# The middle blocks of a feed-forward stage as a hardware loop instead of written out

## The chip, the cores and the metric

The kernel runs on one core of a Trainium2 chip. The metric is the device time of one execution in microseconds (us). Each of the five engines (PE for matmuls, DVE, ACT, POOL, and SP, which only issues transfers here) has its own instruction stream, read by its own sequencer; semaphores order the streams among each other.
## The reference

An input x of shape (2, 2048, 256) in float32 goes through four residual stages, each on a layer-normalised x. Here they are called A, B, C and D:

```
x = x + A(layernorm(x))    # rmsnorm, product with w_qkva, sigmoid gate, scan over time, times q
x = x + F(layernorm(x))    # B: feed-forward
x = x + C(layernorm(x))    # second-order linear attention, 16 heads, then @ W_o
x = x + F(layernorm(x))    # D: the same feed-forward

def F(x, W1, b1, W2, b2):                       # W1 (1024, 256), W2 (256, 1024)
    h = einsum('bsd,fd->bsf', x, ternary(W1)) + b1
    h = gelu(h)                                 # exact, not the tanh form
    return einsum('bsf,df->bsd', h, ternary(W2)) + b2
```

The change touches the code of stage B alone.

## The kernel before

x stays in on-chip memory (`xres`) for the whole run. Rows are taken in blocks of 512, so each of the two batches b has `NBLK` = 4 blocks, and stage B works through eight half-iterations: block i of batch 0, block i of batch 1, then the next i. One *iteration* below is one i, with both batches.

In a half-iteration PE makes eight groups of 128 hidden columns, f = 0 to 7. `up` (L695, L696) is four matmuls of 512 columns for one group, into one of two PSUM banks (`HB`). ACT applies GELU (L758) and then copies the high part (`hid_hi`, L747); DVE subtracts to get the low part (`hid_lo`, L802). `down` (L708, L710), the second product, runs one half-iteration later: eight parts of eight matmuls of 256 columns, woven between the ups from f = 2 on, the last two parts after f = 7. After f = 3 come the eight transposes (L169) of the next half-iteration's normalised rows.

Waits that matter around the change. `up` of group n waits until the GELU of group n-2 has freed its bank (`gelu_done`). GELU waits for its group's matmuls (`h_ready`), for the low part made four groups earlier (`hlow_done`), and, at f = 0, for `out_ready`. The first `down` part waits for all eight low parts of the half-iteration before it. Every count is the sum of a start value and i times a constant, so with i known when the program is built it is a constant.

Each engine's order in stage B comes from one helper, `steps` (L623 to L629), which calls the engine's `iteration` for i = 0, 1, 2, 3 and writes all four out, so that every count and every address of `xres` is a constant. Stage A is built by another helper, `stage_loop` (L270 to L279): it writes i = 0 and i = 3 out and puts i = 1 and i = 2 in a hardware loop `Fori`, in which i is a register of each engine. The rows of stage A therefore show a two-pass loop on the same engines. Stages C and D are written out.

Of the kernel before, what the change touches and what calls it, by code (L numbers as in the profile page):

```python
# [18 lines left out]
NBLK = T // BLK  # L19
# [13 lines left out]
def hybrid_kernel(nc, x_d, gamma_d, wqkva_d, wq_d, wk_d, wv_d, wo_d, w1_d, b1_d, w2_d, b2_d, out_d):  # L33
# [13 lines left out]
    with outer:  # L47
# [558 lines left out]
        def feed_forward(tag, stage, w1t, w2t):  # L606
            with ExitStack() as st:
# [15 lines left out]
                def steps(iteration, tail):  # L623

                    def run(eng):
                        for i in range(NBLK):
                            iteration(i, i == 0, i == NBLK - 1)
                        tail()
                    return run  # L629

# [1071 lines left out]
```

How the kernel before makes its waits and increments, by code:

```python
            def dve_statistics(self, dve, b, i, n):  # L138
                for c in range(CH):
                    nc.vector.bn_stats(ln_stats[:, b, c, :], rows(b, i, c)).then_inc(self.stats_done[b], 1)
                dve.wait_ge(self.stats_done[b], START + (n + 1) * CH)
                nc.vector.memset(ln_filler[:, :], 0.0)
                for c in range(CH):
                    nc.vector.bn_aggr(ln_moments[:, b, c, :], ln_stats[:, b, c, :]).then_inc(self.moments_done[b], 1)
# [1 line left out]
            def pool_rstd(self, pool, b, n):  # L147
                pool.wait_ge(self.moments_done[b], START + (n + 1) * CH)
                nc.gpsimd.tensor_tensor(ln_vare[:, b, :], ln_moments[:, b, :, 1], ln_eps[:, :],
                                        ALU.add).then_inc(self.vare_done[b], 1)
                pool.wait_ge(self.vare_done[b], START + n + 1)
                nc.gpsimd.tensor_tensor(ln_rstd[:, b, :], ln_vare[:, b, :], minus_half[:, :],
                                        ALU.pow).then_inc(self.rstd_done[b], 1)
# [1 line left out]
            def dve_normalise(self, dve, b, i, n, factor):  # L156
                dve.wait_ge(self.transposed[b], START + n * DC)
                for c in range(CH):
                    nc.vector.tensor_scalar(self.xn[:, b, c, :], rows(b, i, c), ln_moments[:, b, c, 0:1],
                                            factor[:, b, c:c + 1], ALU.subtract, ALU.mult)\
                        .then_inc(self.normalised[b], 1)
```

## Time and profile before

| what | value |
|---|---|
| median of 3 runs | 1068.14 us (1068.07 to 1070.59) |
| the profiled execution | 1068.14 us |
| its span, first to last instruction | 1066.4 us |
| stage A, about 0 to 126 us of the span | 126 us |
| stage B, about 126 to 266 us | 140 us |
| stages C and D | 800 us |
| mean granted clock of PE | 0.988 of full speed |

Between the span and the execution's own time lie 1.7 us, which no row shows. Busy time of PE counts matmuls, which overlap one another (a matmul of 512 columns is shown with 0.39 us, and the next starts 0.23 us after it), so the view to read is where each matmul starts, and what sits before the few late ones.

### The profile page before, as it was taken

Reading aid. Unit: us, or ns where it says so; the run is one execution under the profiler, and the core shown is the slowest. Engines: PE = TensorE matmul, PEld = TensorE weight load, DVE = VectorE, ACT = ScalarE, POOL = GpSimd, SP = SyncE. Lnnn points to the kernel's source line nnn. Section 1 sums busy time; section 2 is a strip of 40 time slices with the busy share of each in tenths; the row PEclk is TensorE's granted clock in tenths of the full one; section 3 lists DMA queues with packets and bytes.
Section 4 is the critical chain, followed back from the end, with each engine's and each line's share of the span. In section 5 each row is a group of like instructions: output and inputs, shape, how many; then the busy total and the mean of one; then the engine's idle time right before and its main releaser. Section 6 shows DMA issues by size and latency. Waiting matters only on the chain.

```text
span 1066.4 us, 42059 instructions
## 1 busy us (share of the span) xinstructions
PE 1014.1 (95%) x19150; PEld 917.4 (86%) x19150; DVE 652.2 (61%) x1315; ACT 470.0 (44%) x875; POOL 128.8 (12%) x114
## 2 busy tenths in 40 slices
PE   6799689998999999999999999999999999999998
PEld 5677579898999899899999998999999888888897
DVE  6999698776253564554555465555546446857773
ACT  4222376664334343343343343344344334546663
POOL 2315264122000000000000000000000000112130
PEclk9999899999899999999999999999999999999999
DMA  9100240002142332342343334234233332300101
GB/s 296 54 1 0 56 182 1 1 1 80 68 134 85 123 117 82 103 139 84 101 122 102 102 103 117 91 96 132 91 96 126 104 121 92 105 18 30 41 30 50
DMA packets 60687, 92.74 MB, mean 87 GB/s; under 512 B 7008, under 2 KB 50400, under 8 KB 59488
## 3 DMA queue, kind: packets, MB, share of 16 engines
q1 hardware_dynamic: 60512, 90.07, 26.7%
q8 instruction: 150, 2.46, 1.0%
q14 instruction: 25, 0.20, 0.1%
HBM read 48.63 MB, written 41.42 MB: 84 GB/s over the span
## 4 chain that ended last, share of the span: by engine, by line
PE 72%; DVE 1%; issue 1%; ACT 1%; POOL 0%; POOLq 0%
PE bank L213 7%; PE bank L214 6%; PE bank L215 6%; PE bank L1085 6%; PE bank L1111 5%; PE bank L1096 5%; PE bank L1145 3%; PE bank L1133 3%; PE bank L1122 3%; PE bank L1075 3%; PE bank L1146 3%; PE bank L1147 3%; PE bank L1161 3%; PE bank L1179 3%; PE bank L1180 3%; PE bank L1076 3%
## 5 line engine op out<-in xcount | busy, mean ns | idle before, releaser
L1503 DVE STREAM_TRANSPOSE k<-kt 128x512 f32<-128x512 f32 x64 | 43.4, 697 | 111.0 <-ACT kt L1362 60.7
L1367 ACT COPY qt<-bank 128x512 f32<-128x512 f32 x64 | 37.6, 587 | 151.6 <-PE bank L215 151.6
L1524 DVE TENSOR_TENSOR state_s<-bank,state_s 128x256 f32<-128x256 f32 x124 | 46.6, 419 | 73.0 <-ACT ut L1380 71.0
L1362 ACT COPY kt<-bank 128x512 f32<-128x512 f32 x64 | 37.6, 587 | 119.7 <-PE bank L215 119.7
L213 PE MATMUL bank<-ln_xhi,wk_hi 128*128 128x256 f32 x256 | 76.9, 301 | 4.1 <-POOL state_z L1019 3.4
L1145 PE MATMUL bank<-wo_hi,ot_hi 128*128 128x256 f32 x256 | 75.5, 295 | 0.0
L213 PE MATMUL bank<-ln_xhi,wq_hi 128*128 128x256 f32 x256 | 75.4, 294 | 0.0
L214 PE MATMUL bank<-ln_xlo,wk_hi 128*128 128x256 f32 x256 | 73.5, 287 | 1.0 <-issue 1.0
L215 PE MATMUL bank<-ln_xhi,wk_lo 128*128 128x256 f32 x256 | 73.3, 287 | 0.2 <-issue 0.2
L1517 DVE TENSOR_TENSOR state_z<-bank,state_z 128x512 f32<-128x512 f32 x62 | 39.9, 686 | 53.1 <-PE bank L1133 53.0
L1146 PE MATMUL bank<-wo_lo,ot_hi 128*128 128x256 f32 x256 | 72.2, 282 | 0.0
L214 PE MATMUL bank<-ln_xlo,wq_hi 128*128 128x256 f32 x256 | 72.2, 282 | 0.0
L1147 PE MATMUL bank<-wo_hi,ot_lo 128*128 128x256 f32 x256 | 72.1, 282 | 0.0
L215 PE MATMUL bank<-ln_xhi,wq_lo 128*128 128x256 f32 x256 | 72.1, 281 | 0.0
L802 DVE TENSOR_TENSOR B_hid_lo<-B_hidden,B_hid_hi 128x512 fp32r<-128x512 f32 x64 | 56.3, 902 | 25.5 <-ACT B_hid_hi L747 25.4
L1096 PE MATMUL bank<-qt,state_s 64*64 64x64 f32 x2048 | 69.3, 221 | 1.9 <-issue 1.8
L1414 ACT ACTIVATE D_hidden<-bank,b_sb 128x512 f32<-128x512 f32 x64 | 44.2, 691 | 60.3 <-PE bank L1162 60.3
L1096 PEld LDWEIGHTS bank<-qt,state_s 64*64 64x64 f32 x2048 | 64.4, 135 | 6.4 <-issue 2.5
L1100 PE MATMUL bank<-qt,state_z 64*64 64x64 f32 x2048 | 69.7, 221 | 0.0
L1100 PEld LDWEIGHTS bank<-qt,state_z 64*64 64x64 f32 x2048 | 64.6, 135 | 0.6 <-issue 0.3
L708 PE MATMUL bank<-w2t,B_hid_hi 128*128 128x256 f32 x256 | 63.8, 285 | 0.5 <-DVE B_hid_lo L802 0.5
L710 PE MATMUL bank<-w2t,B_hid_lo 128*128 128x256 f32 x256 | 63.5, 283 | 0.0
(155 smaller groups left out, 2956.5 us busy)
## 6 DMA issues: line engine op xcount, KB each, us to landing
k_rows_scratch<-k SPq DMA_DIRECT2D x32, 512.0 KB, 2.9
k<-k_rows_scratch SPq DMA_DIRECT2D x128, 128.0 KB, 3.5
u_rows_scratch<-sc_and_k SPq DMA_DIRECT2D x31, 512.0 KB, 3.1
landed<-u_rows_scratch SPq DMA_DIRECT2D x124, 128.0 KB, 3.1
out_dram<-xres SPq DMA_DIRECT2D x16, 256.0 KB, 2.1
xres<-in_L_attn_a_x_dram SPq DMA_DIRECT2D x4, 512.0 KB, 7.3
w_nat<-in_L_ffn_W_dram SPq DMA_DIRECT2D x2, 1024.0 KB, 8.9
xres<-in_L_attn_a_x_dram SPq DMA_DIRECT2D x2, 1024.0 KB, 15.2
```

The source lines that it names most:

```text
L213: nc.tensor.matmul(out, w_hi, x_hi, start=(k == 0), stop=False)
L214: nc.tensor.matmul(out, w_hi, x_lo, start=False, stop=False)
L215: return nc.tensor.matmul(out, w_lo, x_hi, start=False, stop=(k == last_k))
L708: nc.tensor.matmul(dst, hid_hi[:, b, f, c * P:(c + 1) * P], w2t[:, f, :], start=(f == 0), stop=False)
L710: last = nc.tensor.matmul(dst, hid_lo[:, b, f, c * P:(c + 1) * P], w2t[:, f, :], start=False, stop=(f == FC - 1))
L802: nc.vector.tensor_tensor(hid_lo[:, b, f, :], hidden[:, f % 4, :], hid_hi[:, b, f, :].bitcast(FP32), ALU.subtract).then_inc(hlow_done, 1)
L1085: last = nc.tensor.matmul(bank[bank_of[h]][half(b), p * CHUNK:(p + 1) * CHUNK], keys(p, h, b), qt[half(h), j // 2 % 2, p, j % 2, b, :], st ...
L1096: last = nc.tensor.matmul(bank[UB[b][p // 4]][half(h), u_cols(p, 0)], state_s[half(h), b, p, :], qt[half(h), j // 2 % 2, p, j % 2, b, :], ...
L1100: last = nc.tensor.matmul(bank[OB[b]][half(1 - h), cols], state_z[half(h), b, p, :], qt[half(h), (j - 1) // 2 % 2, p, (j - 1) % 2, b, :], ...
L1145: nc.tensor.matmul(dst, ot_hi[:, p, :], w[0], start=(p == 0), stop=False)
L1146: nc.tensor.matmul(dst, ot_hi[:, p, :], w[1], start=False, stop=False)
L1147: last = nc.tensor.matmul(dst, ot_lo[:, p, :], w[0], start=False, stop=(p == PAIRS - 1))
```

## The change

`steps` now writes i = 0 out, puts i = 1 and i = 2 in a hardware loop, and writes i = 3 out, for every engine that uses it (PE, ACT, DVE, POOL). SP's program has no such loop.

```
                     def run(eng):
-                        for i in range(NBLK):
-                            iteration(i, i == 0, i == NBLK - 1)
+                        iteration(0, True, False)
+                        with eng.Fori(1, NBLK - 1) as i:
+                            iteration(i, False, False)
+                        iteration(NBLK - 1, False, True)
                         tail()
                     return run
```

The matmuls and other operations, their order and their buffers are the same, and the arithmetic too. What differs is the form in which i reaches them. On ACT, this is the start of iteration i = 1 before (the casts end i = 0; `B_hlow`, `B_h`, `B_out0` are the semaphores `hlow_done`, `h_ready`, `out_ready[0]`):

```order
L770 CAST wk_hi<-B_wqk_raw 128x512 x3
L758 ACTIVATE B_hidden<-bank,b_sb 128x512 [waits B_hlow,B_h,B_out0]
L758 ACTIVATE B_hidden<-bank,b_sb 128x512 [waits B_hlow,B_h]
L747 CAST B_hid_hi<-B_hidden 128x512 [waits B_gelu]
L758 ACTIVATE B_hidden<-bank,b_sb 128x512 [waits B_hlow,B_h]
```

and this is the same place now, two lines lower in the file:

```order
L772 CAST wk_hi<-B_wqk_raw 128x512 x3
L627 UNCONDITIONAL_BRANCH
L627 ISA
L757 ISA [waits B_out0]
L759 REGISTER_ALU [waits B_h]
L760 ACTIVATE B_hidden<-bank,b_sb 128x512 [waits B_hlow]
L757 REGISTER_ALU
L759 REGISTER_ALU [waits B_h]
L760 ACTIVATE B_hidden<-bank,b_sb 128x512 [waits B_hlow]
L749 CAST B_hid_hi<-B_hidden 128x512 [waits B_gelu]
```

Register instructions stand between the operations, and for batch 0, f = 0, the wait for the matmuls sits on one of them, ahead of the GELU. On PE the end of the loop body is this (the last of the down matmuls, then the test of i, then the first up of i = 3, which is written out):

```order
L712 MATMUL bank<-w2t,B_hid_lo 128x256
L627 REGISTER_ALU
L627 COMPARE_AND_BRANCH
L697 MATMUL bank<-ln_xhi,w1t 128x512 [waits B_gelu,ln_low_done0]
```

and the branch leads back once to this, the start of the body:

```order
L627 UNCONDITIONAL_BRANCH
L627 ISA
L694 REGISTER_ALU [waits ln_low_done0]
L697 MATMUL bank<-ln_xhi,w1t 128x512 [waits B_gelu]
L698 MATMUL bank<-ln_xlo,w1t 128x512
L697 MATMUL bank<-ln_xhi,w1t 128x512
L698 MATMUL bank<-ln_xlo,w1t 128x512
L694 REGISTER_ALU
L697 MATMUL bank<-ln_xhi,w1t 128x512 [waits B_gelu]
```

One copy of an iteration fewer stands in each engine's program, and every instruction behind stage B stands that much earlier in it. PE's copy has 208 matmuls, each with its weight load.

## Rows read from the trace of the kernel before

**Rows 1.** The page: busy us, share of the span and instructions of each engine.
```profile
PE 1014.1 (95%) x19150; PEld 917.4 (86%) x19150; DVE 652.2 (61%) x1315; ACT 470.0 (44%) x875; POOL 128.8 (12%) x114
```

**Rows 2.** Busy time by stretch (columns in the first line): a half-iteration of stage B.
```profile
core 0: us, PE busy (x) PEld busy (x) DVE busy (x) ACT busy (x) POOL busy (x), PEclk, DMA share, GB/s
174.05:190.12 16.07, 16.07 (x107) 14.42 (x105) 13.35 (x27) 10.37 (x18) 3.95 (x3) 1.00 0.00 1
```

**Rows 3.** Waits, 175 to 239 us: us in total, times, longest.
```profile
ACT B_hidden L758 <- PE bank L696: 14.3, 20, 1.6
ACT B_hidden L758 <- issue: 8.5, 4, 2.1
PEld bank L695 <- ACT B_hidden L758: 1.4, 4, 0.3
```

**Rows 4.** Timeline at a half-iteration's start: start, us, engine, line, operation.
```profile
174.75 0.40 PE L696 MATMUL bank<-ln_xlo,w1t 128*128 128x512 f32 x1
...
175.23 0.69 ACT L758 ACTIVATE B_hidden<-bank,b_sb 128x512 f32<-128x512 f32 x1 [2.12 <-issue]
...
175.67 0.39 PE L696 MATMUL bank<-ln_xlo,w1t 128*128 128x512 f32 x1
175.97 0.19 PEld L695 LDWEIGHTS bank<-ln_xhi,w1t 128*128 128x128 f32 x1 [0.34 <-ACT B_hidden L758]
```

**Rows 5.** Timeline, stage A: the gate behind its matmuls, written out, then in loop.
```profile
24.85 0.39 PE L215 MATMUL bank<-ln_xhi,wa_lo 128*128 128x512 f32 x1
...
25.28 0.60 ACT L460 ACTIVATE gate<-bank 128x512 f32<-128x512 f32 x1 [1.90 <-PE bank L215]
...
70.14 0.39 PE L215 MATMUL bank<-ln_xhi,wa_lo 128*128 128x512 f32 x1
...
70.64 0.60 ACT L460 ACTIVATE gate<-bank 128x512 f32<-128x512 f32 x1 [5.20 <-PE bank L215]
```

**Rows 6.** Line 275, stage A's loop: duration ns min/median/max, first and last start us.
```profile
L275 PEldq FUSED_REGOPS  x2: 59/59/59, 39.7 to 64.2; - x2
L275 PEldq COMPARE_BRANCH  x2: 83/164/246, 63.9 to 85.2; - x2
L275 DVEq COMPARE_BRANCH  x2: 50/56/63, 67.6 to 88.8; - x2
```

**Rows 7.** Line 692 on PE's sequencer, 186 to 190 us (columns as rows 6).
```profile
L692 PEldq EVENT_SEMAPHORE  x1: 51/51/51, 188.0 to 188.0; - x1
```

**Rows 8.** Transfers in four stretches (46:67, 67:88, 158:190, 354:358): packets, MB.
```profile
q8 instruction: 1, 0.02, 0.4%
...
DMA packets 0, 0.00 MB, mean 0 GB/s; under 512 B 0, under 2 KB 0, under 8 KB 0
...
q8 instruction: 2, 0.03, 0.4%
...
q8 instruction: 1, 0.02, 2.0%
```

**Rows 9.** The page, transfers by queue over the run: packets, MB, share.
```profile
q8 instruction: 150, 2.46, 1.0%
```

**Rows 10.** PE's waits behind no other engine, 268 to 1066 us; then one of them.
```profile
PE bank L1085 <- issue: 2.3, 2, 1.5
PE bank L1096 <- issue: 1.8, 3, 1.3
...
357.50 0.28 PE L1085 MATMUL bank<-qt,kt 64*64 64x64 f32 x4 [1.48 <-issue]
```

**Rows 11.** A long wait of PE in stage B, and the stretch behind it (columns: rows 2).
```profile
141.83 0.50 PE L695 MATMUL bank<-ln_xhi,w1t 128*128 128x512 f32 x1 [2.50 <-ACT B_hidden L758]
...
142.50:145.90 3.40, 2.92 (x12) 2.20 (x11) 3.40 (x3) 1.56 (x3) 3.40 (x3) 0.50 0.57 234
```

**Rows 12.** Timeline, 162 to 164 us: the last normalise, and the transposes that read it.
```profile
162.07 1.38 DVE L160 TENSOR_SCALAR ln_xn<-xres,ln_moments,ln_rstd 128x256 f32<-128x256 f32 x1
...
163.77 0.38 PE L169 MATMUL bank<-ident,ln_xn 128*128 128x128 f32 x2
```

## The prediction

> **What bounds the kernel now.** I read the busy shares first, then the stretches of stage B, its waits, and one half-iteration's start. PE is busy 95% of the span [rows 1]. In the middle of stage B it is busy all the time: a half-iteration takes 16.07 us, of which PE is busy 16.07, at the full clock (2.4 GHz), with ACT at 10.4 and DVE at 13.4 us [rows 2]. So only what makes a matmul start later costs time there. The waits show one such place: in 64 us PE's weight load waits four times for a GELU, 1.4 us in all, once per half-iteration [rows 3]. The timeline shows it: the last matmul of up 0 starts at 174.75 and lasts 0.40, so it ends at 175.15; the GELU follows at 175.23, ends at 175.92, and up 2, which needs that bank back, starts at 175.97. The matmul before it started at 175.67, and the steady step between such matmuls is 0.23 us, so up 2 is 0.07 us late [rows 4]. This chain has no slack: each nanosecond added between up 0 and the end of the first GELU makes PE late by as much, once per half-iteration. The other GELUs have down parts between the ups, and ACT waits for PE there (20 times, 14.3 us [rows 3]), so they have room.
>
> **What the change adds.** No operation is removed, added or moved. Four things change.
>
> *Waits and addresses through registers.* The loop covers i = 1 and i = 2, four half-iterations. On ACT, in the two halves of batch 0, the wait for up 0 stands on a register instruction, and the GELU is sent off behind it. Stage A's loop has just that, and its written-out part has not. Written out, the last matmul ends at 24.85 + 0.39 = 25.24 and the gate starts at 25.28, 0.04 us later; in the loop it ends at 70.53 and the gate starts at 70.64, 0.11 us later [rows 5]. Difference 0.07 us. For f = 0 in stage B before, the distance is 175.23 - 175.15 = 0.08 us [rows 4], since three waits are already divided there, so the difference may be as small as 0.03. I take 0.05 us for two halves = 0.1 us. In the two halves of batch 1 the register instruction waits for the down products, done before up 0; I take nothing. Bounds: 0 (the register instruction hides in the 0.04 to 0.08 that a wait costs anyway) and 0.12 in all four halves, 0.5 us.
>
> On DVE register instructions stand before the normalises, the statistics and the adds. In steady iterations ACT and PE do not wait for DVE at all [rows 3], and its idle time per half is 16.07 - 13.35 = 2.7 us [rows 2]. One place is tight, at the loop's entry: the last normalise ends at 162.07 + 1.38 = 163.45 and the transposes that read it start at 163.77 [rows 12], 0.32 us of room. Entering the loop costs DVE's sequencer one or two register steps (PE's took 59 ns [rows 6]), and it reads ahead while the add before still runs. I take 0; bounds 0 and 0.2 us, once. POOL is busy 3.9 us of 16 and has room.
>
> *The jump back.* It is taken once per engine. In stage A PE's branch took 246 ns when taken and 83 when not, with a register step of 59 ns behind it; DVE's took 63 and 50 ns [rows 6]. A sequencer step costs time only if the sequencer is not ahead of its engine. PE's carried out its wait for the up that runs at 190.12 [rows 2] already at 188.0 [rows 7], 2.1 us ahead. The jump takes from 63.9 to 64.2 + 0.06, about 0.4 us [rows 6], and the first register wait in the body perhaps 0.1: hidden, with 1.6 us to spare. ACT at this place waits 2.1 us for up 0 anyway [rows 3] and jumps inside that wait. On DVE the branch, and as much again for register steps, lies in its 2.7 us. Cost 0; the upper bound, no cover at all, is PE's 0.4 us.
>
> *Instruction loads.* PE's instructions arrive in packets on queue q8, 150 for 2.46 MB [rows 9], 16 KB each; with 2 x 19150 matmuls and weight loads [rows 1] that is about 255 instructions a packet. The loop of stage A (two steps of 52 matmuls, some 220 instructions) loaded one packet during its first pass and none in its second: the stretch 67:88 has no packets at all, of any engine [rows 8]. So a jump back across one packet's boundary loaded nothing. The body in stage B is 208 matmuls with their weight loads and some twenty register instructions, about 440 instructions; in the same stretch before, 158:190, two packets came [rows 8], so the body spans two boundaries and the jump goes back over both. No row shows that. I take it as free as well, from the nearest row; its price if it is not is the second rival's.
>
> *Code behind stage B moves.* One copy of about 420 instructions less, so all of the packets' boundaries fall elsewhere in stages C and D. There PE waits at times behind no engine at all, for instance 1.48 us at 357.50, with one load in that stretch [rows 8, 10]; the two longest rows of this kind make 2.3 + 1.8 = 4.1 us over the 800 [rows 10]. Where the boundaries fall decides which loads come late. The sum has no direction; all of it could go (-4) or as much be added (+4). I take 0, and a spread of 1.5 to 2 us. The three runs themselves differ by 2.5.
>
> Sum: 0.1 + 0 + 0 + 0 = +0.1 us. The profiled execution took 1068.14, which is also the median of the runs, so 1068.2; the small terms' bounds are 0 and 0.5 + 0.2 + 0.4 = 1.1 us, mostly above, so I say 1068.3.
>
> The Trainium skill has a rule against the change: the page "Runtime: NRT & Kernel Launch", section "Instruction fetch mechanics", says that a taken branch whose target is not in the current window of two pages forces a fetch of that page before the engine goes on. By that rule the jump of stage A could stay inside the window, as the trace shows, and that of stage B, two pages back, could not; it would make the second or the third rival below of my forecast.
>
> **The rivals.**
>
> 1. *Forecast*: all of it hidden, 1068.3. For it: the second pass of stage A's loop loads nothing [rows 8], and PE's sequencer is 2.1 us ahead [rows 2, 7]. Against: the longer body.
>
> 2. *The jump back reloads, and is partly covered.* PE's sequencer must fetch a packet before it goes on. The nearest price is a load that came late in stage C, 1.48 us of idle PE where little cover was [rows 10]. So 0 to 1.5 us, 1069.8 at most. The next two boundaries in the body lie some 150 or more instructions on, at 0.12 us and more for a pair of them, and are loaded in time. For it: the body spans two boundaries. Against: nothing in stage A's second pass had to be loaded again.
>
> 3. *The other side: the reload is long enough for the clock to fall.* Place: PE, the start of i = 2. After its idle 2.50 us before 141.83 PE ran at half clock (1.2 GHz) for the 3.40 us from 142.50, its 2.92 us of busy time worth half of that at full clock [rows 11]: a loss of about 1.7 us of the 3.4. If the reload leaves PE idle as long as that wait did, the cost is 2.5 + 1.7 = 4.2 us: 1072.5. It decides when the fetch takes more than the 2.1 us of lead and 2.5 us on top, 4.6 us in all. Against: a late load in stage C showed at most 1.5 us.
>
> 4. *The boundaries in stages C and D.* They fall better, fewer late loads: about -4 us, 1064.3. Or worse: +4, 1072.3. In between, it only shifts the forecast inside its spread.
>
> **How the numbers follow.** About 0.3%, 3.2 us, is what a measurement of this kernel tells from no change. The forecast with small shifts from rival 4: 0.68. Rival 2: 0.15, also inside. Rival 3: 0.08, slower. Rival 4 with a gain over 3.2 us: 0.05; with a loss over 3.2 us: 0.04. So faster 0.05, slower 0.12, within 0.3% 0.83. The range: below, the forecast less 2 us of shift, 1066.3; above, rival 2 at its full price and one more late load of 1.2, 1071.0. That leaves out about 2 in 10.
>
> **What would show it.** The profile after should have half-iterations of 16.1 us through i = 1 and i = 2; the first GELU of batch 0's halves 0.03 to 0.1 us later behind its matmuls; one taken branch on PE of about 250 ns with no gap on PE behind it; and one pass of the loop without any packet on q8, so 148 packets or fewer instead of 150 (with rival 2 they are loaded again and the count stays). PE's waits behind no engine in stages C and D will sit at other places. I am wrong if PE shows a gap over 1 us at the start of i = 2, if a half-iteration inside the loop is over 16.4 us, which would mean that the register waits take PE's lead away, or if the late loads in stages C and D change by more than 3 us.

## The result, and the profile after

The looped kernel took 1078.07 us (median of 9 runs, 1074.74 to 1083.16), the kernel before beside it 1068.65 us (9 runs). The ratio is 1.0087, 95% interval 1.0066 to 1.0106: slower by about 9 us, where 1068.3 and no change had been predicted. The profiled execution took 1076.05 us. Its page has the same work as rows 1 and 9, a span 7.9 us longer, and one packet of instructions less:

```profile
span 1074.3 us, 42245 instructions
PE 1014.4 (94%) x19150; PEld 917.1 (85%) x19150; DVE 652.4 (61%) x1315; ACT 469.4 (44%) x875; POOL 129.4 (12%) x114
...
q8 instruction: 149, 2.44, 1.0%
```

The changed place itself behaves as foreseen. Two half-iterations in the loop, by stretch, as in [rows 2] (16.07 us there):

```profile
core 0: us, PE busy (x) PEld busy (x) DVE busy (x) ACT busy (x) POOL busy (x), PEclk, DMA share, GB/s
173.50:189.50 16.00, 16.00 (x106) 14.40 (x105) 13.16 (x27) 10.35 (x18) 3.94 (x3) 1.00 0.01 2
189.50:205.50 16.00, 16.00 (x105) 14.37 (x104) 12.50 (x25) 10.35 (x18) 3.93 (x3) 1.00 0.00 0
```

The instructions of the loop's line, as in [rows 6], show the branch on TensorE taken at 187.2 in 242 ns, and passed at 219.3 in 83:

```profile
L627 PEldq FUSED_REGOPS  x2: 59/59/59, 154.3 to 187.5; - x2
...
L627 PEldq ALU_OP  x2: 32/32/32, 187.1 to 219.2; - x2
L627 PEldq COMPARE_BRANCH  x2: 83/162/242, 187.2 to 219.3; - x2
```

Transfers of 158:190 and of 190:222, as in [rows 8]: two packets on q8 in the first pass, none of any queue in the second, so the jump over two boundaries loaded nothing again.

```profile
q8 instruction: 2, 0.03, 0.4%
...
DMA packets 0, 0.00 MB, mean 0 GB/s; under 512 B 0, under 2 KB 0, under 8 KB 0
```

The time is lost some 90 us and more behind the loop's end. From TensorE's first matmul of stage B to its first of stage C it took 139.1 us before and 138.0 after; from there to the end of the span 799.9 before and 808.7 after, +8.8. These are the first matmuls of stage C, before and after:

```profile
266.53 0.58 PE L213 MATMUL bank<-ln_xhi,wk_hi 128*128 128x256 f32 x1 [3.45 <-POOL state_z L1019]
```
```profile
265.67 0.39 PE L213 MATMUL bank<-ln_xhi,wk_hi 128*128 128x256 f32 x1 [3.45 <-POOL state_z L1021]
```

The following are TensorE's waits in stages C and D that the profile puts behind no other engine ("issue"). [rows 10] showed 2.3 and 1.8 us as the two largest rows of the kernel before; the looped kernel has:

```profile
PE bank L1087 <- issue: 6.1, 4, 2.0
PE bank L1102 <- issue: 2.8, 4, 1.5
...
PE bank L1147 <- issue: 1.4, 1, 1.4
PE bank L214 <- issue: 1.3, 1, 1.3
PE bank L1098 <- issue: 0.9, 2, 0.5
```

They make 12.5 us; in the kernel before all such waits make 5.9. One of the two longest is a row of the timeline. Behind it, and behind one like it that ends at 607, the clock is at half (1.2 GHz) for 3.4 us (two stretches, columns as above):

```profile
315.49 0.50 PE L1087 MATMUL bank<-qt,kt 64*64 64x64 f32 x17 [1.96 <-issue]
```
```profile
317.20:320.60 3.40, 3.40 (x24) 3.18 (x26) 0.25 (x2) 0.00 (x0) 0.00 (x0) 0.51 0.00 0
607.30:610.70 3.40, 3.40 (x17) 3.40 (x18) 0.63 (x1) 0.00 (x0) 0.00 (x0) 0.51 0.02 5
```

At half clock half of each stretch is lost, an estimate of 3.4 us for the two. More late instructions, 12.5 - 5.9 = 6.6, and the clock, 3.4, are 10.0 us, against 8.8 measured in stages C and D (the table below sums single gaps: 12.4 and 6.0). The missing 1.2 us is in the first microseconds of stage C. Behind its first wait, which both kernels have, the kernel before is at half clock for 5.7 us and the looped one for 3.4 of the 3.6 us shown (columns as above; the clock is the figure after POOL's):

```profile
266.50:272.20 5.70, 5.67 (x26) 5.67 (x27) 0.38 (x2) 0.73 (x2) 0.23 (x1) 0.50 0.00 0
```
```profile
265.70:269.30 3.60, 3.60 (x18) 3.60 (x19) 0.38 (x2) 0.59 (x1) 0.17 (x1) 0.53 0.00 0
```

Half of the difference is 1.1 us less lost in the looped kernel, so 8.9 us are accounted for.

**Counting places.** A packet of 16 KB holds 256 instructions, and a place is an instruction's number, 0 to 255, in its packet. Counting TensorE's weight loads, matmuls and sequencer instructions in the trace from its first of stage C on, every gap "behind no engine" stands where the count passes a multiple of 256, within two instructions, if stage C begins at place 253 of a packet in the kernel before and at place 106 in the looped one. The looped code is some 400 instructions shorter: the shift from 253 to 106 is 147, and with one whole packet 403. Matmuls are numbered from stage C on: after is late at matmuls 967 (1.96 us), 5792, 8455 (1.97), 11119 and others; before at 2039 (1.48), 14342, 15484.

### The profile page after: what moved, and what is told of

Read it like the earlier page. It is cut to its first block, busy times and chain, and to the rows that moved or that the text cites. A ratio compares the mean times of both kernels' runs of the same rounds, so it can differ in the third digit from the quotient of the medians.

```text
span 1074.3 us, 42245 instructions
## 1 busy us (share of the span) xinstructions
PE 1014.4 (94%) x19150; PEld 917.1 (85%) x19150; DVE 652.4 (61%) x1315; ACT 469.4 (44%) x875; POOL 129.4 (12%) x114
## 4 chain that ended last, share of the span: by engine, by line
PE 72%; issue 1%; DVE 1%; ACT 1%; POOL 0%; POOLq 0%
PE bank L213 7%; PE bank L214 6%; PE bank L215 6%; PE bank L1087 6%; PE bank L1113 5%; PE bank L1098 5%; PE bank L1147 4%; PE bank L1135 3%; PE bank L1124 3%; PE bank L1077 3%; PE bank L1148 3%; PE bank L1149 3%; PE bank L1163 3%; PE bank L1181 3%; PE bank L1182 3%; PE bank L1078 3%
```

## The experiments

Theory P: where the packet boundaries fall in stages C and D makes the difference. Rivals: Q, register waits and addresses in the loop; R, the loop on the other engines. (The expectations use further letters; each says what it means.) All results are in one table. Median and ratio are of all executions of a run. The last three columns are read from its one profiled execution: the time from stage C's first matmul to the end; late, the sum of TensorE's gaps at boundaries in stages C and D; half, the stretches of 3.4 us at half clock there, leaving out those at the start of stage C and at the end.

| run | place of stage C | median us | ratio to before, 95% | C + D us | late us | half |
|---|---|---|---|---|---|---|
| before | 253 | 1068.65 | | 799.9 | 6.0 | 0 |
| after | 106 | 1078.07 | 1.0087 [1.0066, 1.0106] | 808.7 | 12.4 | 2 |
| e1 loop on TensorE alone | 106 | 1075.62 | 1.0053 [1.0032, 1.0074] | 810.9 | 14.2 | 2 |
| e2 loop on the others alone | 253 | 1070.08 | 0.9998 [0.9979, 1.0017] | 798.3 | 7.0 | 0 |
| e3 before | 0 | 1070.13 | 0.9997 [0.9982, 1.0012] | 795.9 | 4.4 | 0 |
| e4 after | 0 | 1072.02 | 1.0021 [1.0002, 1.0040] | 799.8 | 4.4 | 1 |
| e5 before | 106 | 1078.13 | 1.0086 [1.0062, 1.0109] | 808.9 | 12.1 | 2 |
| e6 after | 253 | 1069.00 | 1.0002 [0.9988, 1.0017] | 800.1 | 5.7 | 1 |
| e7 before | 24 | 1077.48 | 1.0075 [1.0053, 1.0096] | 808.9 | 11.6 | 3 |
| e8 before | 40 | 1070.39 | 1.0019 [1.0, 1.0039] | 800.6 | 7.4 | 1 |
| e9 before, "worst" | 72, 4 jumps | 1095.53 | 1.0238 [1.0206, 1.027] | 824.6 | 23.7 | 7 |
| e10 before, "best" | 252, 4 jumps | 1078.07 | 1.0077 [1.006, 1.0093] | 810.2 | 12.8 | 1 |
| e11 after, "best" | 252, 4 jumps | 1074.92 | 1.0057 [1.0041, 1.0073] | 804.9 | 10.2 | 0 |
| e12 after, quarter rows | 106 | 1067.29 | 0.9998 [0.9986, 1.0009] | 796.6 | 4.1 | 0 |
| e13 before, quarter rows | 253 | 1062.03 | 0.9943 [0.9924, 0.9962] | 792.5 | 1.2 | 0 |
| e14 "best", quarter rows | 252, 4 jumps | 1065.89 | 0.998 [0.997, 0.999] | 797.6 | 4.6 | 0 |
| e15 after, two at a time | 106 | 1073.59 | 1.005 [1.0027, 1.0073] | 804.4 | 10.8 | 0 |
| e16 before, two at a time | 253 | 1067.19 | 0.9968 [0.995, 0.9987] | 797.2 | 4.1 | 0 |
| e17 before, two at a time | 0 | 1067.44 | 0.9981 [0.9967, 0.9996] | 797.3 | 4.3 | 1 |
| e18 after, few rows | 106 | 1066.96 | 0.9993 [0.998, 1.0006] | 797.4 | 4.9 | 0 |

Take from C + D the late time and 1.7 us for each stretch at half clock, and 789 to 796 us stay in every row. Most of this rest's spread is the half clock at the start of stage C: none in the profiled executions of e2, e3, e8, e9 and e17, 5.3 to 5.8 us in those of before, e4, e10 and e14, 3.4 us in the others. With half of that taken off too, the two kernels and the ten runs with one placing and complete transfers (e1 to e8, e16, e17) keep 790.5 to 791.7 us, e15 792, and all rows 789 to 793. So the late time and the clock carry nearly all of the differences.

**e1 and e2: which engine.** The loop as in the change, but for one engine or for all the others; those left out get the four iterations written out.

```
+if eng.engine == mybir.EngineType.PE:      # e1; != in e2
+    iteration(0, True, False)
+    with eng.Fori(1, NBLK - 1) as i: ...
+else:
+    for i in range(NBLK): ...
```

> The loop in stage B on PE alone; ACT, DVE and POOL have their four iterations written out as before. Theory P (the place of PE's instructions in their 16 KB packets, behind stage B, makes more loads come late in stages C and D): PE's program is that of the changed kernel, so stages C and D take 808 to 809 us as in the changed kernel (800 before), and the time is 1076 to 1079 us. Theory Q (the register forms and the loop on ACT, DVE and POOL, or the place of their code, are what costs): 1068 to 1070 us.

> The counterpart: the loop on ACT, DVE and POOL, PE written out as before. Theory P: PE's program is that of before to the last instruction, so stages C and D take about 800 us and the time is 1068 to 1070 us. Theory Q: 1076 to 1079 us.

e1 is slow with TensorE's loop alone, late at matmuls 967, 5792, 8455, 11119 as after. Its median, 1075.62, is a little under the 1076 to 1079 expected, and 5.5 us above the 1070.14 of the kernel before beside it, where the changed kernel was 9.4 above; the two intervals overlap. e2 is the kernel before in time and nearly in places. Theory R falls.

**e3 to e8: only the place.** One line ahead of TensorE's stage C, which jumps on to the given place of a packet; no operation changes.

```
 def _(pe):
+    pe.addr_align(256, offset=0, max_nops=0)   # e3, e4; 106 in e5, 253 in e6, 24 in e7, 40 in e8
```

> The kernel before with one directive on PE ahead of its stage C code, which places the next instruction at slot 0 of a 256-instruction packet (the padding is jumped over). No loop in stage B. Theory P: the time of stages C and D depends on that slot and on nothing else in stage B; with slot 0 it is anywhere from 795 to 810 us, and the same as in the next run within 1.5 us. Theory R (the loop itself leaves something behind, such as a changed state of the sequencer's buffer): 800 us here and 808 in the next run.

> The changed kernel with the same directive and the same slot 0. Theory P: stages C and D as long as in the run before it, within 1.5 us, with the late loads at the same matmuls; the whole kernel differs from it by under 2 us (stage B alone). Theory R: 8 us longer than it.

> The kernel before, with all twelve passes of stage B written out on every engine and no jump back anywhere; the only edit places the first instruction of TensorE's stage C at place 106 of its packet of 256 instructions, where the looped kernel has it, in place of 253. Theory P (where the packet boundaries of TensorE's code fall in stages C and D makes the whole difference): this kernel is as slow as the looped one, 1075 to 1079 us, ratio 1.006 to 1.010; stages C and D 806 to 811 us against 799.9; late packets ahead of matmuls 967, 5792, 8455 and 11119 of stage C on, as in the looped kernel, and one or two stretches at half clock behind them. Theory L (the loop leaves something behind, in registers, semaphores or the order of arrival at stage C, that places the stalls): nothing is left behind here, so 1067 to 1071 us, ratio 0.998 to 1.002, with stages C and D at 798 to 801 us.

> The looped kernel, with the only edit that TensorE's stage C begins at place 253 of its packet, as in the kernel before. Theory P: the loss goes, though all five engines loop: 1067 to 1071 us, ratio 0.998 to 1.002, stages C and D 798 to 801 us, late packets at the matmuls where the kernel before has them, none at 967. Theory L: 1074 to 1079 us, ratio 1.005 to 1.010, stages C and D 806 us and more.

> The kernel before, stage C of TensorE at place 24 of its packet, one never seen on a chip. Theory P with its count (a packet is asked for when the sequencer enters the one ahead of it, and is there 3.2 us later; matmul times from the run of e3): this is the worst place of all, late packets sum up to 12.7 us against 4.2 at place 0 and 5.3 at 253, so stages C and D 804 to 811 us and the time 1074 to 1080 us, ratio 1.005 to 1.011. If only the place 106 happens to be bad, or the count is wrong, the time is that of the kernel before, 1067 to 1071 us.

> The kernel before, stage C of TensorE at place 40, sixteen instructions behind that of e7. Theory P with its count: late packets sum up to 4.4 us, as little as at place 0, so stages C and D 795 to 799 us and 1066 to 1071 us, ratio 0.997 to 1.001. If an added jump ahead of stage C or any change of place costs by itself, it is as slow as e7.

e5 has no loop in stage B (its four iterations, not twelve passes, are written out) and is as slow as the looped kernel; e6 has the loop on all four engines (not five, as its expectation says) and costs nothing. Stage A's loop is in every run. TensorE's waits in stages C and D, first of e5, then of e6:

```profile
PE bank L1086 <- issue: 4.9, 3, 2.0
...
PE bank L1101 <- issue: 2.2, 2, 1.5
PE bank L214 <- issue: 1.9, 1, 1.9
...
PE bank L213 <- issue: 1.4, 1, 1.4
PE bank L1146 <- issue: 1.2, 1, 1.2
```
```profile
PE bank L1088 <- issue: 2.6, 2, 2.0
...
PE bank L1099 <- issue: 1.4, 3, 0.8
...
PE bank L213 <- issue: 1.0, 2, 0.7
```

Theory P holds and Q falls as the cause of the 9 us: e4 and e6 loop with registers on all four engines and lie 0.21% and 0.02% above before. A cost of the loop itself of up to 2 us isn't excluded: e4 is 1.9 us above e3 at the same place, e6 0.5 us above before. e7 was picked by the count as the worst place, never run before, and is slow (11.6 us late, 12.7 expected). Sixteen instructions further on, e8 is near before (1.9 us above, interval from 0), with 7.4 us late where the count said 4.4. e3 shows 4 us less in stages C and D, but its median equals before's: its profiled execution, 1065.69 us, was the fastest of its ten, and of the 4.0 us only 1.6 are late time; the rest goes with the half clock at the start of stage C, which cost before some 2.8 us and which that execution lacks. So place 0 isn't shown to be better than 253.

**e9 to e11: several places.** The same jump also ahead of four chunks, at places that the count gives as worst and best.

```
+    places = {7: 204, 8: 248, 17: 128, 27: 156}    # e9; {8: 232, 11: 220, 20: 228, 23: 220} in e10, e11
 ...
+    if j in places:
+        pe.addr_align(256, offset=places[j], max_nops=0)
     first_group(j)
```

> The kernel before; TensorE's stage C begins at place 72, and ahead of chunks 7, 8, 17 and 27 its code jumps on to places 204, 248, 128 and 156, which the count gives as the worst with four jumps. Theory P with its count: late packets sum up to 27 us (23 to 31 for 3.0 to 3.4 us to a packet) in place of 5.3, and some of the gaps pass 1.9 us and bring half clock of 3.4 us, 1.7 us each, so stages C and D 818 to 838 us and the time 1088 to 1108 us, ratio 1.018 to 1.037; the largest gaps, over 2 us, stand at the two short packets around chunks 8 and 17. Theory N (only the number of packets and the spread that any program has; places 106 and 24 were bad by another cause): 1068 to 1078 us.

> The kernel before, TensorE's stage C at place 252, and jumps on to places 232, 220, 228 and 220 ahead of chunks 8, 11, 20 and 23, the best that the count finds. Theory P with its count: late packets sum up to 1.1 us (0.6 to 4.4), each jump costs up to 0.25 us, so stages C and D 793 to 797 us against 799.9 and the time 1063 to 1067 us, ratio 0.995 to 0.999. If jumps cost more than the late packets that they save, 1067 to 1071 us.

> The same placing for the looped kernel. Theory P: within 1 us of e10, 1063 to 1068 us, ratio 0.995 to 1.000: the loop then costs nothing. If the loop has a cost of its own beside the placing (e4 read 1.0021, e6 1.0002), 2 us above e10.

e9 came as expected, 26 us above before. The sizes of its gaps were not all where expected: 3.2 us behind the jump ahead of chunk 7 (415.8), 1.2 behind that ahead of chunk 8 (441.1), 2.7 behind 17 and 3.2 behind 27. The longest:

```profile
421.90 0.60 PE L1135 MATMUL bank<-v_all,urow 64*64 64x64 f32 x13 [3.23 <-issue]
```

e10 and e11 missed: 12.8 and 10.2 us late where 1.1 was expected, and e11, expected within 1 us of e10, was 3 us faster, which stays open. So placing makes the time, but the count, which gives every load 3.2 us from the boundary before it, leaves out something that makes packets late. e10's longest gap, and what the DMA engines did between that packet's boundary (773.9) and its load (in 777.0:777.5):

```profile
779.38 0.47 PE L1087 MATMUL bank<-qt,kt 64*64 64x64 f32 x8 [2.11 <-issue]
```
```profile
773.90:777.00 3.10, 3.10 (x122) 2.59 (x124) 1.23 (x3) 2.18 (x4) 0.00 (x0) 1.00 0.76 192
```
```profile
q1 hardware_dynamic: 661, 0.60, 75.7%
```
```profile
q8 instruction: 1, 0.02, 13.8%
q1 hardware_dynamic: 1, 0.00, 0.1%
```

The load started 3.1 us behind the boundary, with row transfers on q1 in between, and the packet's first instruction ran 2.3 us after that. The late packet of after at 967 has the same look. Its boundary is at 308.4; the transfers of 308.4:312.7, and then of 312.7:313.2:

```profile
q1 hardware_dynamic: 699, 1.04, 74.9%
```
```profile
q1 hardware_dynamic: 86, 0.08, 72.7%
q8 instruction: 1, 0.02, 18.1%
```

Over the boundaries of all these kernels with less than 9 us to the next, the load began 0.6 to 0.8 us (median) behind the boundary where the DMA engines were under 0.1 busy in the microsecond after it (some 1200 cases), and 1.5 to 1.7 us where over 0.9 (some 450 cases); the bounds come of how exactly a boundary's time can be read. This goes together and does not yet show a cause.

**e12 to e14, and e18: fewer rows.** Theory D: the row transfers delay the packets. Theory F: the load time is fixed. Only SyncE's transfers are cut (e14 has the jumps of e10 too), so these kernels leave out data and compute something else. Behind the start of stage C q1 moves 72 MB in a complete kernel, 48 in e12 to e14 and 16 in e18.

```
-tile[t * 32:(t + 1) * 32, :, :, :] ... [t]
+n = 1 if count else 4                       # e12, e13, e14
+tile[t * 32:(t + 1) * 32, 0:n, :, :] ... [t][:, 0:n, :]
```

> The looped kernel; from the second landing on, the rows of k and u come back from DRAM with a quarter of their packets (one row block of four; the rest of the rows is left out). Theory D (a packet of instructions is late where it is asked for while the row transfers fill the DMA engines): the gap ahead of matmul 967, 2.0 us, falls below 0.5, late packets in stages C and D sum up to 5 to 9 us in place of 12.5, stages C and D 798 to 804 us, the time 1067 to 1073 us. Theory F (a load takes the same 3.2 us always, and only the density of instructions decides): gaps as before, 1075 to 1079 us.

> The kernel before with the same quarter of the row packets. Theory D: the gaps ahead of matmuls 2039 and 15484 (1.5 and 1.3 us) fall below 0.5, late packets sum up to 1 to 3.5 us in place of 6.1, stages C and D 794 to 798 us, 1062 to 1067 us, and the distance to e12 shrinks from 8.8 to 3 to 7 us. Theory F: 1067 to 1071 us.

> The placing of e10 with a quarter of the row packets. Theory D: the count by a fixed load time now holds, late packets sum up to 0.5 to 4 us in place of some 12, and the time is that of e13 within 3 us, 1062 to 1068 us. Theory F, or a cost of the four jumps: 1074 us and more, as e10.

All three moved the way of theory D, and F falls: nothing was changed on TensorE against after, before and e10. Between the medians of e12 and e13 5.3 us are left of the looped kernel's 9.4. The looped kernel with a quarter of the returning rows, TensorE's waits in stages C and D:

```profile
PE bank L1088 <- issue: 2.5, 4, 0.9
...
PE bank L1103 <- issue: 0.7, 2, 0.4
PE bank L214 <- issue: 0.5, 1, 0.5
PE bank L1148 <- issue: 0.4, 1, 0.4
```

The gap at 967 fell to 0.95 and not below 0.5, and e14 kept 4.6 us, so a rest was open. e18 took nearly all rows away (16 partitions of 128 saved, 16 rows of a block returned).

```
+m = 16 if count else P
+sp.dma_start(scratch[0:m], ...[0:m]) ...
 ...
+n, m = (1, 16) if count else (4, 32)        # rows that come back
```

> The looped kernel; from the second chunk on only 16 of the 128 partitions of each row tile are saved and 16 rows of each quarter's first block come back, so nearly all row traffic of stage C is left out. Theory D (the traffic delays the packets): the gap ahead of matmul 967 falls below 0.3 us, late packets sum up to 0 to 2.5 us in place of 12.4 (4.1 in e12), stages C and D 792 to 795 us, the time 1062 to 1066 us. Theory G (the traffic is only part of it; a packet is also asked for late when TensorE's queue is full of wide matmuls or its sequencer waits): 0.6 us and more are left at 967, some 4 us in all, as in e12, and 1066 to 1068 us.

```profile
PE bank L1089 <- issue: 2.8, 4, 0.8
...
PE bank L1104 <- issue: 1.0, 2, 0.6
PE bank L214 <- issue: 0.8, 1, 0.8
PE bank L1149 <- issue: 0.3, 1, 0.3
```

No better than e12: 4.9 us stay late at place 106, 0.76 at matmul 967, whose load began 3.1 us behind its boundary, with the DMA engines 0.23 busy in that stretch:

```profile
310.90:314.80 3.90, 3.86 (x60) 3.03 (x64) 1.91 (x4) 1.14 (x3) 0.00 (x0) 1.00 0.23 47
```

This was theory G's side. So of the looped kernel's 12.4 us late, some 7.5 to 8.3 and both stretches at half clock need the row transfers, and 4.1 to 4.9 us stay with few of them. The place still counts then: with a quarter of the rows 1.2 us are late at place 253 (e13) and 4.1 at 106 (e12). What holds such a request back in a quiet stretch is open; that it is TensorE's full queue was only supposed.

**e15 to e17: a complete kernel with thinner transfers.** SyncE waits for the first two transfers of a landing before the other two.

```
 for t in range(4):
     sp.dma_start(...).then_inc(landing, 16)
+    if t == 1:
+        sp.wait_ge(landing, 64 * count + 32)
```

> The looped kernel with all its row packets, but SyncE waits for the first two of each landing's four transfers before it issues the other two, so that the DMA engines are less full at a time and the landing takes some 2 us longer. Theory D: the waits for the engines are shorter, the late packets sum up to 8 to 12 us in place of 12.5 and the time is 1071 to 1077 us, if the later rows delay nothing on TensorE. Theory F: 1075 to 1079 us. If the rows come too late for ScalarE, TensorE waits for semaphores and the time is over 1080 us.

> The kernel before, complete, with at most two of a landing's four transfers outstanding. Theory D: late packets sum up to 3 to 5 us in place of 6.1, stages C and D 796 to 799 us, the time 1065 to 1068 us, ratio 0.996 to 0.9995. If the rows that come some 2 us later make TensorE wait, or if the traffic is only spread over more packets, 1068 to 1074 us.

> The same with stage C of TensorE at place 0 of its packet, the best place seen on the chip (stages C and D 795.9 us in e3). Theory D: stages C and D 793 to 797 us and 1063 to 1068 us, ratio 0.994 to 0.9995, so faster than both kernels; otherwise 1068 to 1073 us.

e16 computes everything and is 3 us faster than the kernel before: 0.9968 [0.995, 0.9987], so 1.4 to 5.4 us; the looped kernel is above both. Its stages C and D are 2.7 us shorter, 1.9 of it late time and the rest the shorter half clock at the start of stage C. Its waits of TensorE in stages C and D:

```profile
PE bank L1087 <- issue: 2.0, 2, 1.2
...
PE bank L214 <- issue: 1.1, 1, 1.1
...
PE bank L1102 <- issue: 0.5, 1, 0.5
PE bank L1098 <- issue: 0.4, 2, 0.2
PE bank L213 <- issue: 0.2, 1, 0.2
```

e15 took back 4 us of the looped kernel's loss in stages C and D, more by its two stretches at half clock than by late time (12.4 to 10.8). e17's place 0 added nothing to e16.

## Why the prediction was wrong, step by step

*Waits and addresses through registers, +0.1.* Right in kind. In the looped half at 190 us the last matmul of up 0 starts at 189.94 and lasts 0.40, and the GELU starts at 190.45, 0.11 us behind its end, where it was 0.08 [rows 4]: 0.03 more, in the foreseen 0.03 to 0.1. The like matmul behind it runs at 175.09 and 191.20, 16.11 us apart.

*The jump back, 0.* Right: 242 ns at 187.2, no gap on TensorE in 173.5:205.5.

*Instruction loads at the jump back, 0.* Right, and so rivals 2 and 3 did not come. Transfers 190:222: none. The Trainium skill ("Runtime: NRT & Kernel Launch", "Instruction fetch mechanics") has a target outside a window of two pages fetched again before the engine goes on; TensorE jumped back over two boundaries and loaded nothing, so the measurement decides against it here.

*Rival 3's price.* It called 1.7 us lost of 2.92 us of busy time; half of 2.92 is 1.5, and 1.7 is half of the whole stretch of 3.4. Nothing hung on it.

*"Code behind stage B moves", taken as 0 with a spread of 1.5 to 2 and ends of -4 and +4.* **This is the step that failed**: it was +8.8 us. The mechanism was named, and rival 4's bad end, 1072.3 with 0.04, was the right side at half the size. Two things were wrong in it. First, the bound: the late loads of the kernel before were summed, and it was supposed that a shift could at most double them or take them away. Nothing in the trace bounds them from above: with the place alone changed in the kernel before they went from 4.4 (e3) to 12.1 us (e5), the loop at the same place gave 12.4 and 14.2 (e1), and e9 with four jumps reached 23.7. Of the five places tried 0, 253 and 40 are good and 24 and 106 bad; the kernel before stood at a good one, so there was more to lose than to win. Second, the half clock was charged to the jump (rival 3) and not to longer late loads, though [rows 11] gave its price: two stretches, 3.4 us. The trace of before also held what was needed to see that the place matters [rows 8 to 10]: a boundary every 256 instructions, of which parts with 64x64 matmuls use two for each matmul. The smallest distance of two loads on q8 was 3.4 us there as well. The sum had no sign because the places were not counted; they can be, from the code and the trace. Whether a count made ahead would have given the right size isn't shown: it foretold e7 and e9 and missed e10 and e11.

Of the marks given at the end, those of stage B were met: half-iterations of 16.1 us, a taken branch of 242 ns without a gap, a pass without packets. The last, wrong "if the late loads in stages C and D change by more than 3 us", was met too: they changed by 6.6. Packets fell to 149, not to 148.

Stage B was 1.1 us shorter in the profiled run. The kernel before has a stretch at half clock there [rows 11] that after lacks; e2 (looped but for TensorE) has it and e5 (no loop in stage B) does not, so it isn't the loop's doing.

## What to carry to other kernels

Shortening or lengthening code on the engine that bounds the kernel moves every packet boundary behind it; where that engine takes small instructions densely, count at which instructions the boundaries fall before and after, and compare those stretches, before calling the edit free. A kernel change that comes out 1% off in a part it did not touch should be repeated with that part's code set to the old place: one line told code from placement here. Late packets are worse beside dense transfers, so spreading these (e16) can pay more than looking for a lucky place (e10). Where a difference is read from one profiled execution a kernel, see which of its executions that was: e3's was the fastest of ten.

## What the runs showed of the hardware

- One packet holds 256 instructions of TensorE. The first instruction of a late one ran 2.2 to 2.8 us after its transfer on q8 began, in nearly all cases (183 of the 188 gaps over 0.15 us in all runs), and no two loads in stages C and D started less than 3.2 us apart (3.36 in the kernel before, 3.21 in e14). Of some 140 boundaries in stages C and D, 10 cost over 0.1 us in the kernel before and 13 in the looped one. The Trainium skill ("Runtime: NRT & Kernel Launch", "Instruction fetch mechanics") calls the cost of crossing a 16 KiB boundary mostly hidden: true of most boundaries here, and those that are not cost 4 to 24 us of a complete kernel all the same.
- Moving code by 16 instructions (e7 against e8) changed the time by 7 us.
- Where row transfers keep the DMA engines over 0.9 busy, loads start about 1 us later at the median, and 4.9 us behind the boundary at the worst seen (e1, matmul 967).
- TensorE fell to half clock (1.2 GHz) for 3.4 us behind 15 of the 16 gaps of 1.87 us and more at late packets in stages C and D, and behind 5 of the 13 of 1.56 to 1.83 us. Around e9's gap of 3.23 us it was 6.8 us, from 1.0 us ahead of the gap's end on; e9's gap of 3.05 us was the one without, and the wait of 1.6 us for VectorE near 910 us, which every run has, never brought it.
- A jump over the rest of a packet costs well under 1 us, an estimate: without late time and all half clock e3, with one jump, keeps 791.5 us in stages C and D, e10 and e11, with five, 792.8 and 793.0, and e9, with five as well, 789.0.
